# The last of four replacements in a top-32 search becomes a ScalarE mask, and the order tables are redone

## What is computed

```python
Q = (x_text @ Wq).reshape(Bb, Tt, H, DH)                  # 8 x 512 x 4 x 32
K = (x_vision @ Wk).reshape(Bb, Gg, H, DH)                # 8 x 1024 x 4 x 32
scores = jnp.einsum('bthd,bghd->bhtg', Q, K) / np.sqrt(DH)
scores = jnp.where(vision_mask[:, None, None, :], scores, -jnp.inf)
topv, topi = jax.lax.top_k(scores, K_TOP)                 # K_TOP = 32 of 1024
probs = jax.nn.softmax(topv, axis=-1)
attn = jnp.zeros_like(scores).at[bi, hi, ti, topi].set(probs)
attn_mean = attn.mean(axis=1)                             # over the 4 heads
V = x_vision @ Wv
c_t = jnp.einsum('btg,bgd->btd', attn_mean, V) * text_mask[..., None]
...
```

## Time and profile before

| | us |
|---|---|
| median of 3 runs | 1795.5 |
| the 3 runs | 1794.97 to 1796.42 |
| span of the profiled execution | 1792.4 |
| DVE busy | 1484.0 (83%) |
| PE busy | 1401.2 (78%) |
| POOL busy | 1195.8 (67%) |
| ACT busy | 1109.9 (62%) |

### The profile page before, as it was taken

The page is one execution under the profiler, slowest core; times in us unless marked ns, Lnnn a source line. Parts: engine busy times, 40 slices in busy tenths (PEclk is TensorE's granted clock), DMA queues, the critical chain, the costliest instruction groups (busy, mean ns, idle before and its releaser), DMA issues.

```text
span 1792.4 us, 20766 instructions
## 1 busy us (share of the span) xinstructions
PE 1401.2 (78%) x6243; PEld 983.5 (55%) x6251; DVE 1484.0 (83%) x2102; ACT 1109.9 (62%) x2362; POOL 1195.8 (67%) x1341
## 2 busy tenths in 40 slices
PE   5566658778876887688888878887887778887896
PEld 3243435455544554456565647664655465655796
DVE  7999999998999999989998999999998995112221
ACT  3789844866485648565986588657865676134442
POOL 1499838577857785688678966896688668624232
PEclk7666778878887888799998999898989989998998
DMA  7200121012001200213322322233222201663232
GB/s 210 65 4 4 35 53 50 24 34 67 7 24 43 58 15 17 51 46 95 97 55 65 100 76 54 57 86 100 53 57 65 91 16 53 202 194 108 61 51 27
DMA packets 97218, 115.15 MB, mean 64 GB/s; under 512 B 17840, under 2 KB 74168, under 8 KB 96964
## 3 DMA queue, kind: packets, MB, share of 16 engines
q1 hardware_dynamic: 85348, 100.32, 19.2%
q0 software_dynamic: 11760, 13.52, 4.9%
HBM read 75.48 MB, written 19.58 MB: 53 GB/s over the span
## 4 chain that ended last, share of the span: by engine, by line
DVE 57%; PE 14%; issue 10%; POOL 8%; ACT 7%; DMA 2%; SPq 1%; POOLq 0%; DVEq 0%; ACTq 0%
DVE R L1422 20%; DVE ZB L1425 16%; DVE ZB L1418 7%; DVE R L1414 6%; DVE R L1379 2%; ACT ZB L1007 2%; PE PS L1969 2%; DMA out<-R 2%; PE PS L2083 2%; ACT R L1013 2%; POOL ZB L731 1%; PE PS L1991 1%; POOL R L910 1%; PE PS L2056 1%; ACT R L1007 1%
## 5 line engine op out<-in xcount | busy, mean ns | idle before, releaser
L1422 DVE MAX8 R<-ZB 128x8 f32<-128x1024 f32 x384 | 471.3, 1227 | 12.2
L1425 DVE MATCH_REPLACE8 ZB<-R,ZB 128x1024 f32<-128x1024 f32 x384 | 464.1, 1209 | 0.0
L731 POOL TENSOR_TENSOR ZB<-ZB 128x1024 f32<-128x1024 f32 x96 | 231.6, 2412 | 94.9 <-ACT ZB L1007 85.6
L1010 ACT ACTIVATE R<-PS 128x512 f32<-128x512 f32 (+6 forms) x404 | 178.1, 469 | 175.3 <-PE PS L2064 28.7
L733 POOL TENSOR_TENSOR ZB<-ZB 128x1024 f32<-128x1024 f32 x96 | 226.3, 2358 | 7.5
L1007 ACT ACTIVATE R<-R 128x32 f32<-128x32 f32 (+4 forms) x356 | 96.4, 275 | 197.4 <-DVE R L1422 172.1
L1414 DVE MAX8 R<-PS 128x8 f32<-128x1024 f32 x128 | 156.2, 1221 | 1.1 <-PE PS L1720 1.1
L1418 DVE MATCH_REPLACE8 ZB<-R,PS 128x1024 f32<-128x1024 f32 x128 | 155.5, 1215 | 0.0
L1013 ACT ACTIVATE R<-R 128x1 f32<-128x1 f32 (+1 forms) x384 | 140.8, 391 | 20.0 <-POOL R L718 15.3
L1007 ACT ACTIVATE ZB<-ZB,R 128x1024 f32<-128x1024 f32 x128 | 146.3, 1143 | 0.3 <-DVE ZB L1425 0.2
L1007 ACT ACTIVATE ZB<-PS,R 128x1024 f32<-128x1024 f32 x128 | 142.7, 1114 | 4.2
(11 more groups left out here) (248 smaller groups left out, 3030.0 us busy)
## 6 DMA issues: line engine op xcount, KB each, us to landing
ZR<-ZR SPq DMA_DIRECT2D x96, 128.0 KB
ZB<-in_L_ffn_rt_gate SPq DMA_DIRECT2D x21, 512.0 KB, 4.2
ZB<-in_L_ffn_rt_up SPq DMA_DIRECT2D x21, 512.0 KB, 5.0
ZB<-in_L_ffn_rt_down SPq DMA_DIRECT2D x21, 512.0 KB, 6.3
R<-in_x SPq DMA_DIRECT2D x16, 512.0 KB, 4.8
ZB<-in_ctx SPq DMA_DIRECT2D x8, 768.0 KB, 5.2
R<-xs_d SPq DMA_DIRECT2D x39, 128.5 KB, 2.1
out<-R SPq DMA_DIRECT2D x32, 128.0 KB, 2.0
```

Source lines behind the costliest of these rows:

```text
L731: pool.tensor_tensor(e, e, w, ALU.subtract).then_inc(s.g_att, 1)
L1010: return act.activation(o, i, ACT.Copy, **k)
L1422: vec.max(ml[:, 8 * r:8 * r + 8], w).then_inc(s.v_tk, 1)
L1425: vec.match_replace(w, ml[:, 8 * r:8 * r + 8], w, NEG).then_inc(s.v_tk, 1)
```

## The change

1. **The search loses its eighth pass.** DVE still does four MAX8, but three replacements. `w` after the third MAX8 round holds all scores but the 24 largest; it is only read by the fourth MAX8.
2. **ACT makes a mask in its place.** `ml[:, 31:32]` is the 32nd score. ACT writes `w = relu(ml[31] - score)` from PSUM (128x1024), which is 0 at the 32 and positive elsewhere, and then `w = exp(-STEEP * w + ln(1 / sum))` in place, which is 1/sum at the 32 and 0 elsewhere. POOL multiplies `e` and `w` where it subtracted. `e` no longer needs the sum, and so may be made before the search ends.
3. **Short values move from ACT to DVE.** ACT loses three 128x1 operations for each tile; DVE gains two: a multiplication of the first maximum by -SCALE, and a reciprocal of the sum. They are a generator of their own, `limits`.
4. **Normalization.** The context tile gets a 193rd column of ones (`CW = DV + 1`), so that the product with `acc` also gives the row's sum. DVE takes the reciprocal, times 4 and the query mask (`shares`, two 128x1 operations for each of the 32 blocks), and ACT applies it as it copies the result out. The query mask no longer enters the exponent.
5. **Two streams.** DVE's search is two generators, one for even and one for odd tiles, each with a semaphore of its own (`v_tk0`, `v_tk1`), with a slot for each pass (`DVE_TOP`).
6. **All slot tables are new.** Many entries are negative by hundreds: such a step comes directly behind its predecessor in its generator.

PE's scores of tile `n` wait for ACT's relu of tile `n - 2`, the last reader of the banks, where they waited for `e`. The parts of the diff stand in the order POOL, ACT, DVE, PE.

```diff
-POOL_SUM = (5.4, -0.8, 5.9, -2.1, 8.1, 15.1, 11.7, 8.4, 9.3, 9.2, 1.2, 0.1, 7.1, 9.1, 2.8, 11)
+POOL_SUM = (110.4, 109.5, 106.4, 79.7, 92.5, 86.8, 80.3, 73.8, 66.4, 58.7, 47.9, 43.9, 36.5, 28.6, 20.9, 1.4)
...
-                    on.wait_ge(s.a_att, 7 * n + 7)
+                    on.wait_ge(s.a_att, 5 * n + 5)
...
-                        pool.tensor_tensor(e, e, w, ALU.subtract).then_inc(s.g_att, 1)
+                        pool.tensor_tensor(e, e, w, ALU.mult).then_inc(s.g_att, 1)
...
-                    yield tile_at(n) + ACT_MAX[n % 16]
-                    on.wait_ge(s.v_tk, 8 * n + 1)
-                    copy(q[:, 0:1], ml[:, 0:1], scale=-SCALE).then_inc(s.a_att, 1)
-                    on.wait_ge(s.v_tmb, 1)
-                    affine(q[:, 1:2], ml[:, 0:1], scale=-SCALE, bias=tmb[:, 4 * b + i:4 * b + i + 1]).then_inc(s.a_att, 1)
                     yield tile_at(n) + ACT_EXP[n % 16]
-                    on.wait_ge(s.v_tk, 8 * n + 7)
-                    on.wait_ge(s.a_att, 7 * n + 1)
-                    exp(junk, ml, ACT.Exp, bias=q[:, 0:1], scale=SCALE, accum_out=q[:, 2:3]).then_inc(s.a_att, 1)
-                    on.wait_ge(s.a_att, 7 * n + 3)
+                    on.wait_ge(s_tk[n % 2], PASS * (n // 2) + 2)
+                    on.wait_ge(s.v_limit, 2 * n + 1)
+                    on.wait_ge(s.g_att, added(n - 2))
+                    exp(e, sc_bank(n), ACT.Exp, bias=q[:, 0:1], scale=SCALE).then_inc(s.a_att, 1)
+                    yield tile_at(n) + ACT_SUM[n % 16]
+                    on.wait_ge(s_tk[n % 2], PASS * (n // 2) + 7)
+                    exp(junk, ml, ACT.Exp, bias=q[:, 0:1], scale=SCALE, accum_out=q[:, 1:2]).then_inc(s.a_att, 1)
+                    yield tile_at(n) + ACT_GAP[n % 16]
+                    act.activation(w, sc_bank(n), ACT.Relu, bias=ml[:, 31:32], scale=-1.0).then_inc(s.a_att, 1)
+                    yield tile_at(n) + ACT_CUT[n % 16]
+                    on.wait_ge(s.v_limit, 2 * n + 2)
                     exp(q[:, 3:4], q[:, 2:3], ACT.Ln).then_inc(s.a_att, 1)
...
-                    exp(w, w, ACT.Exp, bias=q[:, 4:5], scale=SCALE).then_inc(s.a_att, 1)
+                    exp(w, w, ACT.Exp, bias=q[:, 3:4], scale=-STEEP).then_inc(s.a_att, 1)
...
-            def attention():
+            def attention(odd):
+                for n in range(odd, 16 * B, 2):
+                    ml, w, at = mx[n % 3], tk[n % 2], DVE_TOP[n % 16]
...
+                    for r in range(1, 4):
+                        yield tile_at(n) + at[2 * r]
+                        on.wait_ge(s_tk[n % 2], PASS * (n // 2) + 2 * r)
+                        vec.max(ml[:, 8 * r:8 * r + 8], w).then_inc(s_tk[n % 2], 1)
+                        if r < 3:
+                            yield tile_at(n) + at[2 * r + 1]
+                            on.wait_ge(s_tk[n % 2], PASS * (n // 2) + 2 * r + 1)
+                            vec.match_replace(w, ml[:, 8 * r:8 * r + 8], w, NEG).then_inc(s_tk[n % 2], 1)
+
+            def limits():
                 for n in range(16 * B):
...
+                    yield tile_at(n) + DVE_LIMIT[n % 16][0]
+                    on.wait_ge(s_tk[n % 2], PASS * (n // 2) + 1)
+                    on.wait_ge(s.a_att, 5 * (n - 3) + 2)
+                    TS(q[:, 0:1], ml[:, 0:1], -SCALE, None, ALU.mult).then_inc(s.v_limit, 1)
+                    yield tile_at(n) + DVE_LIMIT[n % 16][1]
+                    on.wait_ge(s.a_att, 5 * n + 2)
+                    vec.reciprocal(q[:, 2:3], q[:, 1:2]).then_inc(s.v_limit, 1)
...
-            weave(setup(), attention(), prep(), weights(), kernel_rows(), post(), tiles(), routed())
+            weave(setup(), attention(0), attention(1), limits(), shares(), prep(), weights(), kernel_rows(), post(), tiles(), routed())
...
-                    on.wait_ge(s.a_att, 7 * (n - 2) + 6)
+                    on.wait_ge(s.a_att, 5 * (n - 2) + 3)
...
-                        ins = pe.matmul(q_bank("finish", t, 2)[:, 0:192], att[:, g, :], cb[b % 2][:, g, :], start=g == 0, stop=g == 7)
+                        ins = pe.matmul(q_bank("finish", t, 2)[:, 0:CW], att[:, g, :], cb[b % 2][:, g, :], start=g == 0, stop=g == 7)
```

253 lines of the change are left out of this document (134 added, 119 removed), and 14 rows, old and new, of tables (DVE_TOP, POST_AT).

## The result

| | before | after |
|---|---|---|
| median | 1796.0 us (4 runs) | 1770.3 us (4 runs) |
| all runs | 1795.0 to 1798.1 | 1767.6 to 1772.9 |
| after / before | | 0.986, 95% interval 0.984 to 0.987 |
| forecast | | 1663.5 us (1628 to 1712) |

The change saves 26 us where 132 were forecast; the time lies 58 us above the upper end of the range. The sign was right, the size was not.

The account below looks back on a forecast made before the run. The prediction took DVE's search, 95% busy, as the bound: span 1792.4 - 155 (DVE) + 1 (head) + 2 (end) + 20 (new waits) = 1660.4 us, plus 3.1 around it, 1663.5 us; range 1628 to 1712.

Parts of the forecast that it names:

- The eighth pass: DVE's search: dropping the fourth replacement saves 1.33 us per tile, 170 us, all on the path.
- short operations and two streams: DVE: added 128x1 operations cost 23 and 9 us; alternating streams with short operations between hide dependences, winning 17 us.
- ACT's work: ACT: relu and mask add 51 us of busy time, not on the path while ACT reaches each sum in time.
- The rival in which ACT comes late at the reciprocal by a table load: DVE's reciprocal: 1.28 us late in half of 88 tight places, 56 us, about 1720 us; chance 0.09.
- The new waits: Three chains leaving a tile's end: +20 us taken, bounded by -33 and +58.
- (a): DVE's reciprocal waits for ACT's sum, maybe 0.7 us late; over 30 us of waits would mean underrated.
- (b): The next first replacement in `w` waits for POOL's product: 5.1 us and five handovers, against 9 us or more mostly.
- (c): PE's scores wait for ACT's relu, 1.5 us after the tile's end; tight in 24 tiles.
- PE's limit: Rival: PE becomes the bound at 85.4% busy, late periods win 1 us each, about 1702 us; chance 0.20.
- The late periods: Late periods of 16 tiles in DVE's search: expected near 167 us, from 183.3.
- Head and end: Before the first MAX8 +1 us for rounding passes; behind the last scores +2 us at most; the end's 285 us stay.
- Slower than before: Rival: DVE waits for ACT at all 88 tight reciprocals, about 1860 us at 2.5 us each; chance 0.06.

Follow-up runs that it names:

- e1: Kernel before, old order, with the fourth replacement left out and nothing in its place (last 8 of 32 get no attention); 1745.8 us, ratio 0.972.
- e2: Kernel before, old order, one search stream, with ACT's relu and mask in place of the fourth replacement, full output; 1805.2 us, ratio 1.005.
- e5: Kernel after with the exponential `e` over 512 of 1024 columns from the third tile on; 1772.2 us, ratio 0.984.
- e6: Kernel after with ACT's mask exponential over 512 of 1024 columns; 1769.3 us, ratio 0.985.
- e10: Kernel after with relu reading `w`, so that PE's next scores wait for `e` and not for relu; 1776.9 us, ratio 0.991.
- e13: Kernel after with ACT's logarithm and mask of a batch's ninth tile ahead of six GELU passes; 1788.1 us, ratio 0.995.
- e15: Kernel after with the moves of e13 and e14, and POOL's table work behind the product of the next batch's first tile; 1824.1 us, ratio 1.015.
- e4: Kernel after with the feed-forward's and shared experts' first products 256 columns wide for 512, from batch 1 on; 1761.4 us, ratio 0.981.
- e18: e17 with e13's move of the ninth tile's logarithm and mask ahead of six GELU passes; 1788.9 us, ratio 0.996.
- e12: Kernel after with DVE's second rounding of the long convolution's kernel moved behind the first five steps of the first search tile; 1781.4 us, ratio 0.992.
- e3: Kernel after with the fourth MAX8 over 512 of 1024 scores; 1764.8 us, ratio 0.983.
- e8: Kernel after with POOL's addition of a head to `acc` over 512 of 1024 columns; 1742.7 us, ratio 0.970.
- e14: Kernel after with DVE's two router steps later in its list, by one pass and by four; 1783.8 us, ratio 0.992.
- e7: Kernel after with POOL's product over 512 of 1024 columns; 1753.5 us, ratio 0.976.
- e9: Kernel after with the cuts of e3, e4, e6, e7 and e8 together; 1701.8 us, ratio 0.948.
- e11: Kernel after with two of the three layer norms behind the attention applied with constants, not waiting for statistics; 1754.5 us, ratio 0.978.
- e17: Kernel after with the first head's product kept in `e` and `acc` first written by the second head's addition; 1770.3 us, ratio 0.986.

## Why the prediction was wrong

**The eighth pass: right in size, and the first step that failed.** Fourth MAX8 to the next tile's first is 683.09 - 681.94 = 1.15 us in the timeline above (forecast 1.14), and DVE's own pace fell by 150.7 us for 155, with short operations and two streams in it. That it came so close is partly luck: the pass alone is worth 162 us by e1 for 170, and so short operations and streams together cost 11 for 15. I had called myself wrong if a short operation held up the passes around it by more than 0.2 us; L1464 did in 8 places, for 7.1 us in all. What failed is the sentence "All of it lies on the path, since DVE is full there". e1 shows it alone: 51 us of 170, with DVE's waits 115 us longer. DVE was full, but the others were only some 50 us behind; the waits of 37 us in the old trace don't say how far.

**ACT's work: a term put at nothing.** The busy time was 39 us more for 51, and relu took 1.10 us, with the next pass mostly 1.00 behind its start, for 1.02. But I costed it at nothing, because ACT had 30% of the search free and stood 172 us at the sum. e2 against e1 shows +59 us for 141 us of relu in the old order, the later handover to PE's scores included. Those 172 us were waits of a list, and a list is late when what stands ahead in it waits for a third engine. ACT's waits for the fourth MAX8 have gone down to 35.3 us in 26 places. That cutting `e` or the mask gives nothing (e5, e6) doesn't contradict it: a pass cut in place doesn't bring forward what stands behind the next wait. The rival in which ACT comes late at the reciprocal by a table load (1.28 us) in 44 places wasn't it either: DVE waits there 14.7 us in 20 places.

**The new waits: +20 forecast, +120 measured.** This is the term of the sum in which the error shows; e1 has 115 of it without any new handover. (a) The reciprocal: 14.7 us, below the 30 that I had named, so by itself not underrated. (b) POOL's product: 46.5 and 15.8 us, 62 where 17 had been; this was the largest. (c) Scores: 23.2 us, 22 more than before (7.2 of them at one tile), but e10 shows that the handover from relu isn't the reason in this order. What I had left out is the router: 36.1 us where 15.9 were, two waits that no part of the change touches. They grow, I take it, because the search no longer covers the way over PE. I had bounded the term from above by +58, by a share of PE's busy time. The measured 120 us are twice that bound, and e13 to e15 show the waits changing with the order alone, from 166 to 202 us: they depend on what stands ahead in each list.

**PE's limit: its sign came true, its reason didn't.** I had said it would be right if PE stays under 87% busy while late periods last 175 us or more. They last 178.8 to 183.8 with PE at 155.12 / 178.8 = 86.8%. Yet with PE at 81% (e4) they last as long, and the end reaches 126.14 / 142.4 = 88.6%, above the 85.4% that I had called the densest. A sign that two theories share is no test. At single places PE's work does hold the search: after's PE is busy without a gap from 687.2 us until the scores of tile 11 at 704.8 (e18 shows what follows).

**The late periods** were to fall to 167 us and stayed. Why they are 8 to 13 us longer than the three before them isn't settled: neither PE's lighter work (180.8) nor the constants in the norms (181.3 and 180.4) changed it, and the experts' weights and gathers, which only run there, weren't tried.

**Head and end.** The end kept its length: -1.7 us for +2. The head cost 8.6 us for 1. The term was read at the rounding pass. But PE's first scores are ready at 67.9 us, and were at 51.5, when DVE only came to them at 59.9: they come 16 us later, behind other products that stand ahead of them in PE's list. e12 shows that moving the rounding pass doesn't help, so it is PE's list in the head that I should have read.

**Slower than before** was a rival with one mechanism, ACT late at 88 reciprocals. It didn't happen. But e2, the same mask in the old order, is slower than before.

**What is shown and what is not.** Shown: the saved time turned into waits of DVE (156.8 us for 36.6); waits of this size come without the mask and in the old order (e1); the mask with its handovers costs time on the path (e2); no engine's amount of work decides by itself (e3 to e8); at one place three reasons stand one close behind the other, two handovers and PE's own work, and each removed one is replaced by the next (e13, e18); a move at one place closes a circle at another (e14). Argued only: that all of the 120 us have this nature, and which part of relu's 59 us is ACT's time. Open: how little time another order could reach. No version here beats both kernels with the full output: those that are faster than after (e1, e3, e4, e7, e8, e9, e11) leave part of it out.

## What to carry to other kernels

When one engine is nearly full, its small waits tell nothing about how close the others are. Take its work away in an experiment first (here the pass alone, 51 us of 170 forecast) before the gain is counted in full. An engine with 30% idle time isn't free for another pass: look at what stands ahead of the step in its in-order list and whom that waits for. And where a kernel's order was fitted to its work, a wait that one step causes can have others a microsecond or two behind it, so that moving single steps can make it slower (here 8 to 49 us) though each move looks right in the trace.

## What the runs showed that was not expected

- On one chip the kernel before repeats within 5 us (1794.7 to 1799.7 in nine runs) and the kernel after within 13 (1771.4 to 1784.0 in four). Over two chips its eight runs lie between 1767.6 and 1784.0; the run of 1784.0 had a granted clock of 0.857, the one of 1767.6 of 0.862. Which of the two moves first, clock or handovers, isn't known.
- With narrower products on TensorE the granted clock fell from 0.859 to 0.834, and products that weren't touched took 402 ns for 389 (L1787) and 599 for 592 (L1951).
- The fourth period lasted 170.5 to 170.9 us in nine kernels with different work or single waits (after, e3, e4, e5, e6, e10, e11, e12, e17), and 174.2 in the slowest run of the kernel after itself.
- A DVE operation of 128x1 with two inputs took 0.16 us at most places and up to 2.35 us where POOL was at work on a 128x1024 product or sum; it then ended within 0.02 us behind POOL's.
